# Column and row tiles of TensorE for the small sums of an eight-stage layer stack, with value products and expert weights moved to earlier places

## What is computed

```python
x = x + tanh(g_xattn[0]) * _L0_xattn_ref(ctx_1024, layernorm(x), ...)     # state-space scan
x = x + tanh(g_ffn[0])   * _L0_ffn_ref(layernorm(x), A, B, Wr, br)        # 8 low-rank experts
x = x + tanh(g_xattn[1]) * _L1_xattn_ref(layernorm(x), ctx_1024, ...)     # 16 heads of 128
x = x + tanh(g_ffn[1])   * _L1_ffn_ref(layernorm(x), ...)                 # ternary weights
x = x + tanh(g_xattn[2]) * _L2_xattn_ref(layernorm(x), ctx_1024, ...)     # 32 heads of 8
x = x + tanh(g_ffn[2])   * _L2_ffn_ref(layernorm(x), ...)                 # 8 experts, top 2
x = x + tanh(g_xattn[3]) * _L3_xattn_ref(layernorm(x), ...)               # int8 smooth-quant
x = x + tanh(g_ffn[3])   * _L3_ffn_ref(layernorm(x), ...)                 # fp8 feed-forward
```

```python
# _L1_xattn_ref: 2 sequences of 512 queries and 512 context rows, H = 16 heads, D = 128
q = (hidden_states @ Wq).reshape(B, Sq, H, D)
k = (encoder_hidden_states @ Wk).reshape(B, Skv, H, D)
v = (encoder_hidden_states @ Wv).reshape(B, Skv, H, D)
q = q * rsqrt(mean(square(q), -1) + eps) * gq
k = k * rsqrt(mean(square(k), -1) + eps) * gk
attn = softmax(einsum('bqhd,bkhd->bhqk', q, k) / sqrt(D), axis=-1)
out = einsum('bhqk,bkhd->bqhd', attn, v).reshape(B, Sq, H * D) @ Wo
```

## Time and profile before

| | |
|---|---|
| median of 3 executions | 1207.11 us (1201.44 to 1210.61) |
| the profiled execution, its own time | 1201.22 us |
| its span in the trace | 1199.5 us |
| mean granted clock of TensorE | 0.891 |
| PE, DVE, ACT, POOL busy | 76%, 57%, 49%, 26% |
| lora stage in the trace | 177.4 to 228.2 us |
| a16: norm, key stage, query loop | 228.2 to 238.0, to 304.6, to 577 us |
| a32 stage | 685.3 to 870.2 us |
| moe stage | 870.2 to 1066.5 us |

### The profile page before, as it was taken

The page is one execution under the profiler, slowest core; times in us unless marked ns, Lnnn a source line. Parts: engine busy times, 40 slices in busy tenths (PEclk is TensorE's granted clock), DMA queues, the critical chain, the costliest instruction groups (busy, mean ns, idle before and its releaser), DMA issues. The chain is left out here.

```text
span 1199.5 us, 15723 instructions
## 1 busy us (share of the span) xinstructions
PE 908.2 (76%) x4836; PEld 553.4 (46%) x4836; DVE 686.3 (57%) x1299; ACT 586.3 (49%) x1118; POOL 314.0 (26%) x228
## 2 busy tenths in 40 slices
PE   4465658799899999999388574988834999914467
PEld 1122225544577777777156462222432666612235
DVE  5799996744344444334648666788360234137686
ACT  3433331389667776766255354677511443212243
POOL 0566630000122222222032144000001666312122
PEclk8689998999999999999789887799966999956679
DMA  2221103222000000000000100000096332230001
GB/s 85 72 88 70 53 1 140 62 61 62 18 14 17 13 18 14 17 17 5 4 1 1 33 17 1 2 3 2 2 355 246 66 74 46 31 101 0 1 1 36
DMA packets 47078, 55.46 MB, mean 46 GB/s; under 512 B 6360, under 2 KB 39904, under 8 KB 47024
## 3 DMA queue, kind: packets, MB, share of 16 engines
q1 hardware_dynamic: 40528, 46.63, 11.7%
q0 software_dynamic: 4416, 6.03, 3.0%
q10 hardware_dynamic: 2080, 2.10, 0.6%
HBM read 48.19 MB, written 6.49 MB: 46 GB/s over the span
## 5 line engine op out<-in xcount | busy, mean ns | idle before, releaser
L1020 POOL TENSOR_TENSOR a_prob<-a_prob,a_inverse 128x512 f32<-128x512 f32 x64 | 66.5, 1039 | 281.0 <-DVE a_inverse L1087 281.0
L1073 DVE TENSOR_REDUCE a_bias<-bank 128x2 f32<-128x512 f32 x64 | 44.3, 692 | 111.8 <-PE bank L823 111.8
L1825 DVE TENSOR_REDUCE a_tops<-bank 128x4 f32<-128x1024 f32 x64 | 77.9, 1225 | 25.5 <-PE bank L1523 22.8
L298 PE MATMUL bank<-ssm_seen,ident 128*128 128x512 f32 x128 | 63.9, 623 | 37.4 <-DVE ssm_seen L474 37.4
L2010 PE MATMUL bank<-moe_wup,moe_xT 128*128 x184 | 84.5, 603 | 8.6 <-issue 7.9
L400 POOL TENSOR_TENSOR ssm_drive<-ssm_du,ssm_b_row 128x1024 f32<-128x1024 f32 x32 | 75.1, 2350 | 33.5 <-DVE ssm_state L464 33.5
L366 ACT ACTIVATE bank<-ssm_delta,ssm_a_neg 128x510 f32<-128x510 f32 x64 | 44.1, 690 | 79.1 <-DVE ssm_state L464 77.7
L1678 ACT ACTIVATE a_prob<-bank,a_exp_scale 128x1024 f32<-128x1024 f32 x64 | 70.9, 1111 | 23.9 <-PE bank L1543 23.6
L464 DVE TENSOR_TENSOR_SCAN ssm_state<-bank,ssm_drive 128x512 f32<-128x512 f32 x64 | 74.8, 1210 | 7.5 <-POOL ssm_drive L400 4.9
L2237 DVE TENSOR_TENSOR moe_act_f<-bank,moe_silu 128x512 f32<-128x512 f32 x23 | 15.9, 692 | 102.9 <-ACT moe_silu L2073 91.2
L968 ACT ACTIVATE a_prob<-bank,a_bias,a_q_factor 128x256 f32<-128x256 f32 x128 | 70.9, 559 | 4.8 <-DVE a_bias L1080 3.8
(11 more groups left out here) (422 smaller groups left out, 2164.7 us busy)
## 6 DMA issues: line engine op xcount, KB each, us to landing
ssm_b_row<-ssm_b_spill SPq DMA_DIRECT2D x16, 512.0 KB, 3.5
moe_wup<-in_l_up_dram SPq DMA_DIRECT2D x8, 1024.0 KB, 15.0
a_wq<-in_l1x_q_dram SPq DMA_DIRECT2D x32, 128.0 KB, 2.1
moe_wdn<-in_l_down_dram SPq DMA_DIRECT2D x8, 512.0 KB, 13.1
a_wo<-in_l1x_o_dram SPq DMA_DIRECT2D x16, 128.0 KB, 2.1
X<-in_x_dram SPq DMA_DIRECT2D x1, 1024.0 KB, 6.4
lora_raw<-in_l_gate_dram SPq DMA_DIRECT2D x1, 1024.0 KB, 7.9
lora_raw<-in_l_up_dram SPq DMA_DIRECT2D x1, 1024.0 KB, 10.0
```

Source lines behind the costliest of these rows:

```text
L298: last = pe.matmul(bank[:, 4 + 2 * k + h, :], core.ident[:, :], seen[:, k, h * HALF:(h + 1) * HALF], start=False, stop=m >= STEPS - CC, sk ...
L1020: pool.tensor_tensor(prob[:, j, :, :], prob[:, j, :, :], inverse[:, j, :].unsqueeze(2).to_broadcast([P, 2, SEQ]), ALU.mult).then_inc(S["p_ ...
L1073: dve.tensor_reduce(bias[:, j, :], bank[:, 2 + j, :].rearrange("p (q n) -> p q n", q=2), AX.X, ALU.max, negate=True).then_inc(S["top"], 1)
L1825: dve.tensor_reduce(tops[:, f // 2 % 3, :, first:first + 2].rearrange("p q h -> p h q"), bank[:, at:at + 2, :].rearrange("p h (q n) -> p h ...
```

## The change

It has six parts.

1. **Router logits as column tiles** (lora and moe). `wR` is padded to 32 columns (a memset on POOL), and the 1024 tokens are four column tiles of 256: tile j writes partitions 32j to 32j+31 of bank 7. ACT copies the bank to `l_rows`, PE transposes it twice, and DVE reads the logits there. The load of `wR` now waits for POOL (`padded`).
2. **Early loads for a16.** At the end of lora's loads, SP also fetches a16's value and output weights, context and key weights, into buffers held over both stages.
3. **Value products in the norm.** The 16 products `wvo` stand at the start of PE's program in a16, ahead of the norm's transposes, and ACT brings them in 8 copies of two heads, around the roots and ahead of `norm_bring`.
4. **The key stage by pairs.** Four key products go through a ring of 3 banks; ACT squares all four halves and brings the even ones (times gain), DVE brings the odd ones. The sums of a pair are 4 column tiles in one bank, so that one Ln and one Exp serve the pair. Each of the four rows of factors is then spread over the partitions by a row tile (`pick`, L809), and DVE multiplies `keys` in place by the four banks. The loop is written out.
5. **The query sums.** They are 4 column tiles of 32 x 128, the Ln and Exp take 128 x 128, a transpose on PE (`turn_factor`, L850) and a copy of 128 x 4 on DVE (`factor`) follow. `query_sums(n+1)` moves on PE from behind `turn(n,0)` to ahead of `scores(n,1)`, and `query_factor` moves on ACT from behind `exps(n,1)` to ahead of `high_part(n,0)`.
6. **Three experts a stage ahead.** SP fetches experts 0 to 2 in a32, whose `prob`, `q_stack`, `k_stack` and `ctxT` now lie in the room of the later experts. In moe SP fetches the other five, and `wR` and `rank8` go to ACT's queue, behind the store of x.

```diff
@@ lora, PE (moe has the same form)
-                for t in range(NT):
-                    for c in range(DC):
-                        last = pe.matmul(lgp[:, t, :], core.xnT[:, c, t * P:(t + 1) * P], wR[:, c, :],
+                for c in range(DC):
+                    for j in range(4):
+                        last = pe.matmul(bank[32 * j:32 * (j + 1), 7, 0:SEQ], wR[:, c, :], core.xnT[:, c, j * SEQ:(j + 1) * SEQ],
                                          start=c == 0, stop=c == DC - 1)
...
                 hidden(0)
+                pe.wait_ge(l_brought, 1)
+                for h in range(2):
+                    last = pe.transpose(bank[:, 4, h * P:(h + 1) * P], l_rows[:, h * P:(h + 1) * P], core.ident[:, :])
@@ a16, PE: value products and key stage
+                for g in range(NH // 2):
+                    await_count(pe, S["vo_ready"], g - 3)
+                    for k in range(2):
+                        last = pe.matmul(bank[:, 4 + g % 4, k * DM:(k + 1) * DM], core.wvT_in[:, 2 * g + k, :],
+                                         core.wo_in[:, 2 * g + k, :], start=True, stop=True)
+                    last.then_inc(S["vo_done"], 1)
                 s.norm_tensor(pe)
...
+                def sums_of(g):
+                    pe.wait_ge(S["k_squared"], 4 * g + 4)
+                    await_count(pe, S["k_logs"], g)
+                    for j in range(4):
+                        last = pe.matmul(bank[32 * j:32 * (j + 1), 7, :], core.ones[:, 0:32], k_sq[:, :, j * SEQ:(j + 1) * SEQ],
+                                         start=True, stop=True)
+                def spread_of(g):
+                    pe.wait_ge(S["k_rows"], g + 1)
+                    await_count(pe, S["key_ready"], 4 * g)
+                    for j in range(4):
+                        rows = slice(32 * j, 32 * (j + 1))
+                        last = pe.matmul(bank[:, 3 + j, :], pick[rows, :], k_row[rows, :], start=True, stop=True)
+                for g in range(1, PAIRS):
+                    for n in range(4 * g, 4 * g + 4):
+                        keys_of(n)
+                    spread_of(g - 1)
+                    sums_of(g)
@@ a16, ACT: key stage
+                for g in range(PAIRS):
+                    for h in range(2):
+                        n = 4 * g + 2 * h
+                        square(n)
+                        bring_keys(n)
+                        square(n + 1)
...
+                    factors(g)
@@ a16, query loop
@@ PE
-                        last = pe.matmul(bank[:, 6 + p, j:j + 1], q_sq[:, j * P:(j + 1) * P], core.ones[:, 0:1],
-                                         start=True, stop=True)
+                        last = pe.matmul(bank[32 * j:32 * (j + 1), 6 + p, 0:P], core.ones[:, 0:32],
+                                         q_sq[:, j * P:(j + 1) * P], start=True, stop=True)
...
                         mix(n - 1, before, 1)
+                    if after is not None:
+                        query_sums(n + 1, 1 - p)
                     scores(n, m, p, 1)
                     turn(n, 0)
                     if after is not None:
-                        query_sums(n + 1, 1 - p)
+                        turn_factor(n + 1, 1 - p)
@@ ACT
                         bring_mix(n - 1, 1)
+                    if after:
+                        query_factor(n + 1, 1 - p)
                     high_part(n, 0)
                     exps(n, p, 1)
-                    if after:
-                        query_factor(n + 1, 1 - p)
@@ DVE
                     scale_top(n, p, 1)
+                    if after:
+                        factor(n + 1, 1 - p)
                     bring(n, 0)
@@ a32, SP
+                for e in range(EARLY):
+                    load_expert(sp, core, e).then_inc(S["experts_in"], 16)
+                    load_expert_back(sp, core, e).then_inc(S["experts_in"], 16)
@@ moe, ACT
                 act.dma_start(x_rows[0:NTOK, :].rearrange("(t p) n -> p t n", p=P), core.X[:, :, :]).then_inc(x_stored, 16)
+                act.wait_ge(padded, 1)
+                act.dma_start(wR[:, :, 0:NE], d["l2_gate"].rearrange("(c p) e -> p c e", p=P)).then_inc(loaded, 16)
+                act.dma_start(rank8[:, :], d["rank8"]).then_inc(loaded, 16)
```

More of the change, by code:

```diff
@@ L779, in two_heads @@
[L779 to L788 removed]
+                pe.wait_ge(core.vo_in, 2 * 16)
@@ L1114, in add @@
                     last.then_inc(S["added"], 1)
+                factor(0, 0)
                 unit(0, 0, False)
```

345 lines of the change are left out of this document (193 added, 152 removed).

## The result

The changed kernel takes 1218.57 us (median of 7 runs, 1216.53 to 1222.08). The kernel before took 1203.14 us in the 7 runs that stand beside it. The ratio is 1.0113, with an interval of 1.0086 to 1.0140: the change makes the kernel slower by about 1.1%. I had forecast 1201 us. The changed profile has a span of 1217.4 us and an own time of 1219.11 us, against 1199.5 and 1201.22.

The account below looks back on a forecast made before the run. PE's program and a chain over all engines were taken as equally tight in the query loop; +2 (lora), -13 (key stage), +13.6 (loop), -8 (moe) gave -5.4, from the 1207.1 median to 1201 us, range 1182 to 1218.

Parts of the forecast that it names:

- What bounds the loop: Query step of 8.29 us: 4.58 through all engines to turn(n,1), then 3.71 of PE without a gap, where additions cost fully.
- The rival in which less work on PE counts: Query loop: PE's own program is the bound, -9 us in 31 steps, total 1180; shares chance 0.30 with nearly free tiles.
- The price of the sums in that place: Column tiles between mix(n-1,1) and scores(n,1): 0.42 us a step, +13 us in 31 steps (6.5 to 27).
- PE idles some 3 us ahead of the queries, as before, and the clock held then: End of a16's key stage: the wait resembles the 2.66 us of before, so no clock loss was counted.
- the prediction's last sentence: Signs of being wrong: tiles don't overlap, POOL's chain doesn't bound the step, or the clock falls somewhere new.
- Key stage: a16 before the query loop: ACT's cycle sets 5.9 us a pair, queries start at 291 to 291.5, -13 us (-17 to +24).
- Lora: Lora stage: shorter logits lengthen PE's wait for masked rows by 1.6 to 4.6 us, clock falls, +2 us (0 to 5).
- The early loads in a32 cost nothing: a32: SP's first rows to place come 52 us after the stage's start and the experts need 12, so 0 us.
- Moe: Moe stage: fewer expert loads and earlier logits let up(0) start at about 905.3; -8 us taken (-5.5 to -11).
- the rival: Moe: wR lands late behind the store of x, so the gain is 5.5 and not 8, total 1204; chance 0.17.
- The slower rival: Sums ahead of scores(n,1) cost 0.86 us a step, tiles one after another with drains; +27, total 1223; chance 0.13.
- the forecast's -5.4: Whole kernel: sum of +2 lora, -13 key stage, +13.6 loop and -8 moe.

Follow-up runs that it names:

- experiment 3: Changed kernel with the four column tiles of the query sums computed twice in a row: 9.10 us a step, one time of 1226.88 us.
- experiment 7: Changed kernel with the old four 128 x 1 matmuls ahead of scores(n,1), their factor on ACT ahead of the high part: 9.23 us a step, 1232.12 us.
- experiment 1: Changed kernel with the query loop of the kernel before (four 128 x 1 matmuls behind turn(n,0), old factor): 1196.32 us, ratio 0.9949 to the kernel before.
- experiment 2: Changed kernel with the query sums' column tiles behind turn(n,0), factor, transpose and copy moved back too: 8.33 us a step, one time of 1195.94 us.
- experiment 4: Changed kernel with unread matmuls where PE idled, in lora and at the key stage's end: 1211.39 us, ratio 1.0060 to the kernel before.
- Experiment 6: Kernel before with only the query sums' part of the change: 1226.02 us, ratio 1.0189 to the kernel before.
- experiment 5: Changed kernel with moe's router weights and rank table first on SP's queue, and a32's experts behind its own five loads: one time of 1209.36 us.
- experiment 9: Changed kernel with tiles behind turn(n,0), unread matmuls, small loads first, and moe's next-stage loads held until the first gathered tile is turned: 1184.59 us, ratio 0.9856.

## Why the prediction was wrong, point by point

**What bounds the loop: right.** The prediction said that the first part of a step hides 0.8 us of PE work and the second hides nothing. Experiments 3 and 7 show the second (0.218 for one more set of 0.21, and 0.87 for 0.82 of matmuls), experiments 1 and 2 the first: with tiles or with the old sums behind the turn the step is 8.33 to 8.37. The rival in which less work on PE counts is refuted by experiment 2: there the sums hold PE for 0.36 us and not 0.82, and the new transpose adds 0.11, but the step is the 8.33 of the kernel before.

**The price of the sums in that place: mis-sized.** The first step of the prediction that failed is "The query sums have half the columns, 0.21, and change twice, 0.2: 0.42 us". The array's 0.21 was right (experiment 3: 0.218). The changes cost 0.34 and not 0.2: 0.24 of it is PE's own, and 0.10 is the later end of the scores. The a32 row from which I took 0.1 a change ended at the next instruction's start, so it could not show that the instruction behind the change also finishes 0.1 later, and in this place DVE's maximum waits for exactly that instruction. In 31 steps the difference is 4 us: 17.0 and not 13.

**"PE idles some 3 us ahead of the queries, as before, and the clock held then": wrong, and the largest miss.** I compared only the last wait. Ahead of it the changed kernel has another, for the last factors, with 1.9 us of work between the two, and the clock fell in that work. The term was put at nothing, though the prediction's last sentence names a clock that falls somewhere new as a sign of being wrong. The loop's start lost 5.4 us (2.8 to the first scores, 2.6 in the first step beyond the step's own growth), and experiment 4, with the clock at 1.00, gave 4.4 of them back. The 1.0 that is left stands at full clock: 0.7 is the first factor's longer way to the first scores (4.79 against 4.12), for which the prediction had 0.6, and the rest is in the first step. The last mix and the last products behind it took 1.7 us more at half clock, after the same waits (0.85 and 1.41 us) that left it at 1.00 in the kernel before; no run settles why. Experiment 6 shows that the key stage's tail is not the only way to lose the clock here: with the old key stage it fell in the first step, too.

**Key stage: mechanism right, size off.** Tiles run side by side, ACT's cycle sets the pace. The copies with a scale hold ACT 0.57 and not 0.48 and come twice, so a pair takes 6.14 and not 5.9, and the first one 6.48: 2.0 us in seven periods. (The terms that the prediction lists for a pair make 5.6, not 5.9; they have five of ACT's six squares and copies.) The first sums were done 1.4 us later than I had worked out, since they ran at half clock (1.94 us for 1.06), and the last spread ran at half clock, too, and took 0.9 more. Together that is 4.3 us. From the forecast's own place of the queries, 291 to 291.5, to the measured one it is 3.9 to 4.4. In the other profiles with this key stage the queries start 65.4 to 67.6 us into a16, so the gain is 9 to 11 us.

**Lora: right in kind.** I had 4.6 us of idle time, and it was 8.64. The logits took 1.07 us where they had taken 5.47, so 4.4 less and not 1.6. The row that I had used holds 17 of the logits' 32 instructions, and lora's own row of before was at hand:

```profile
185.83 5.47 PE L556 MATMUL bank<-lora_wR,xnT 128*128 128x8 f32 x32 [1.25 <-ACT xnT L161]
```

The first two hidden tiles took another 1.4 us less, at full clock. The loss was 3.2 us, of which experiment 4 gave back 2.1.

**"The early loads in a32 cost nothing": wrong.** I looked at the rows that SP places at 737 and not at the stage's own last load, which the experts follow. It landed 1.5 us later relative to the stage's start (8.3 against 6.8), DVE's bound waited for it, and the stage lost 3.5 us. Holding the experts back gave back all of it (experiment 5). How 1.5 us became 3.6 by the first maximum can be read from the two timelines. The second round of products (at 722.03) ran at half clock for longer, which cost another 0.9. The last 32 transposes took 3.56 us at a clock of 0.51, behind a wait of 2.79, and before they took 2.37 at 1.00, behind a wait of 2.78: 1.2 more. All six profiled kernels in which the experts come ahead of that load show a long row of these transposes (3.3 to 3.6 us) and a stage of 186.9 to 191.1 us; the five without it have 183.2 to 184.4. Why the clock fell behind the same wait stays open.

**Moe: the rival was the case.** The rank table landed 12.7 us after its issue, and the logits came 4 us later than before. The gain was 4.6 us in the stage, close to the rival's 5.5. What I had not priced was ACT's time to issue three transfers ahead of its table load, 2.5 us. And once the logits are early, the tile is bound by something I had not named: its gather shares the queues with loads for later stages. Experiment 5 freed the logits and won only 2 us at the first product; experiment 9 took the loads away and won 3.3 more there. One reading was off, though no term rests on it: 369 GB/s over 44.6 us are 16.5 MB, not 18.

**The range and the sum.** The slower rival had the right place, and its point of decision, 0.59 us a step, was nearly reached by 0.55. Its mechanism, tiles one after the other, was not the case (experiment 3), so a time close to its 1223 does not speak for it. No single term turned the sign. The 23.3 us between the forecast's -5.4 and the traces' +17.9 are: 6.1 at half clock at the loop's two ends, 4.0 for the price of the sums, 0.4 more in the first step, 3.8 in the key stage, 3.5 in a32, 3.4 in moe, 1.2 in lora and 0.9 elsewhere. All have one sign: I had summed single values for terms that had more room on the slow side. The 1201 was also helped by chance. It starts from 1207.1, the median of three times of the kernel before, and the median of seven is 1203.1; from there the same -5.4 would have given 1198.

## What to carry to other kernels

In a loop where two chains are equally long, an operation's price depends on where it stands: the same four matmuls cost nothing behind a turn that another engine's chain covers, and 0.87 us ahead of the scores that start that chain. Before moving work, ask which instruction the chain waits for, and put nothing ahead of it. When a change makes PE faster in a stretch, count all idle time that this leaves there, as the clock may fall and take the gain back in the next stretch. And when a big load is moved to an earlier stage, look for the small load that it now stands beside or ahead of.

## What was unexpected of the hardware

- A set of column tiles between full-array matmuls cost 0.34 us beyond its array time: 0.24 on PE, and 0.1 as a later end of the matmuls behind it (1.13 against 1.03 us). By the Trainium skill a change of tiling mode drains the engine (TensorEngine Tiling (Array Packing), Key Properties): the 0.24 agrees with it, and so does experiment 3, where a second set without a change added only 0.218. The later end does not tell: it stood behind the old matmuls of 128 x 1 as well (1.11).
- The length of a wait does not tell by itself whether the clock falls. It fell to 0.50 behind a wait of 1.95 us at the end of the new key stage, and stayed at 1.00 behind one of 2.66 us at the end of the old one. In a32 it stayed at 1.00 behind 2.78 us before and was 0.51 behind 2.79 us in the changed kernel. Dummy matmuls in the waits of lora and of the key stage kept it at 1.00 and won 6.4 us in all.
- A transfer of 4 KB issued behind a store of 1 MB and beside 8 MB of weights landed after 12.7 us; first in line, on SP's queue, it took 4.7. Its issue alone held ACT for 1.92 us.
